# Key tiles of the exponentials added on GpSimd, weight sums two beats behind the scores

## The reference

```python
L = jnp.einsum('bhqd,bhkd->bhqk', q, k) * scale
mask = jnp.tril(jnp.ones((t, t), dtype=L.dtype))[None, None]
k_y = _split_heads(x @ w_ky.T)
L_y = jnp.einsum('bhqd,bhkd->bhqk', q, k_y) * scale
agg = jnp.sum(jnp.exp(jnp.clip(L_y, -15.0, 15.0)) * mask, axis=-1, keepdims=True) + EPS
r = _eml(L, agg)                       # log(|L| + eps) - log(agg + eps)
w = jax.nn.softplus(r) * mask
A = w / (jnp.sum(w, axis=-1, keepdims=True) + EPS)
out = jnp.einsum('bhqk,bhkd->bhqd', A, v)
```

## Time and profile before

| what | value |
|---|---|
| median of 3 runs | 1399.82 us |
| the profiled execution: its time, its span | 1398.2 us, 1396.4 us |
| TensorE matmul busy | 1280.9 us (92%) |
| VectorE, ScalarE busy | 718.2 us (51%), 614.8 us (44%) |
| GpSimd busy | 113.3 us (8%) |
| granted TensorE clock, mean | 0.972 |

### The profile page before, as it was taken

The page is one execution under the profiler, slowest core; times in us unless marked ns, Lnnn a source line. Parts: engine busy times, 40 slices in busy tenths (PEclk is TensorE's granted clock), DMA queues, the critical chain, the costliest instruction groups (busy, mean ns, idle before and its releaser), DMA issues.

```text
span 1396.4 us, 22945 instructions
## 1 busy us (share of the span) xinstructions
PE 1280.9 (92%) x8310; PEld 817.6 (59%) x8310; DVE 718.2 (51%) x1223; ACT 614.8 (44%) x810; POOL 113.3 (8%) x140
## 2 busy tenths in 40 slices
PE   5888999999898989977399999999999999999996
PEld 1433444434343434433278778787787878878785
DVE  2456777677676776566243532535326353353523
ACT  3566666666666666655042322323223241232411
POOL 1111121111111121110000000000000000000000
PEclk8999999999999999998589999999999999999998
DMA  2002222132122221000290000000000000000000
GB/s 74 16 16 69 92 75 77 60 102 78 60 90 90 90 71 57 1 31 31 70 331 15 16 15 15 30 15 19 11 15 30 15 30 0 15 30 15 30 0 16
DMA packets 31943, 66.89 MB, mean 48 GB/s; under 512 B 2848, under 2 KB 8608, under 8 KB 31904
## 3 DMA queue, kind: packets, MB, share of 16 engines
q1 hardware_dynamic: 31904, 66.35, 14.3%
HBM read 46.42 MB, written 19.92 MB: 48 GB/s over the span
## 4 chain that ended last, share of the span: by engine, by line
issue 50%; POOL 0%; DVE 0%; POOLq 0%; DVEq 0%
POOL f_rstd L809 0%; DVE f_res L816 0%; POOLq L909 0%; DVEq L821 0%; POOL f_minus_half L907 0%; POOLq L83 0%
## 5 line engine op out<-in xcount | busy, mean ns | idle before, releaser
L935 ACT ACTIVATE f_h_full<-f_layer_bank,f_scales 128x512 f32<-128x512 f32 x128 | 88.0, 687 | 354.8 <-PE f_layer_bank L1049 354.7
L500 DVE TENSOR_TENSOR w_ring<-score_banks,keep 128x1024 int32<-128x1024 int32 (+1 forms) x192 | 191.6, 1040 | 46.9 <-PE score_banks L649 46.9
L353 ACT ACTIVATE e_ring<-score_banks 128x1024 f32<-128x1024 f32 (+1 forms) x192 | 158.8, 879 | 122.8 <-PE score_banks L649 122.0
L1049 PE MATMUL f_layer_bank<-f_ha_hi,f_w_all 128*128 128x512 f32 x512 | 204.7, 400 | 2.7 <-DVE f_h_full L977 2.3
L1049 PE MATMUL f_layer_bank<-f_hb_hi,f_w_all 128*128 128x512 f32 x512 | 202.8, 396 | 0.0
L1049 PE MATMUL f_layer_bank<-f_ha_lo,f_w_all 128*128 128x512 f32 x512 | 202.1, 395 | 0.0
L1049 PE MATMUL f_layer_bank<-f_hb_lo,f_w_all 128*128 128x512 f32 x512 | 202.0, 395 | 0.0
L491 DVE TENSOR_SCALAR e_ring<-e_ring 128x2048 f32<-128x2048 f32 (+1 forms) x96 | 100.5, 1046 | 122.3 <-ACT e_ring L353 122.3
L360 ACT ACTIVATE w_ring<-w_ring 128x2048 f32<-128x2048 f32 (+1 forms) x96 | 156.8, 1633 | 8.6 <-DVE w_ring L500 8.3
L287 POOL TENSOR_SCALAR_AFFINE_SELECT e_ring<-e_ring 128x512 f32<-128x512 f32 (+1 forms) x96 | 78.5, 818 | 516.5 <-DVE e_ring L491 516.5
L675 PE MATMUL acc_bank<-w_ring,v_aug 128*32 128x512 f32 (+3 forms) x1024 | 91.2, 452 | 27.8 <-ACT w_ring L360 27.8
(11 more groups left out here) (101 smaller groups left out, 1535.0 us busy)
## 6 DMA issues: line engine op xcount, KB each, us to landing
piece<-in_wf SPq DMA_DIRECT2D x44, 256.0 KB, 2.9
wf_copy<-piece SPq DMA_DIRECT2D x44, 256.0 KB, 3.0
f_w_all<-wf_copy SPq DMA_DIRECT2D x2, 4096.0 KB, 26.4
f_x_turn<-x SPq DMA_DIRECT2D x9, 512.0 KB, 3.2
xq<-in_xt SPq DMA_DIRECT2D x8, 512.0 KB, 3.3
xv<-in_xt SPq DMA_DIRECT2D x8, 512.0 KB, 3.3
res<-in_xn SPq DMA_DIRECT2D x8, 512.0 KB, 4.6
x<-res SPq DMA_DIRECT2D x8, 512.0 KB, 2.6
```

Source lines behind the costliest of these rows:

```text
L353: nc.scalar.activation(e_ring[:, t % RING, 2 * i:2 * i + 2, 0:cols], pair_banks(y_pair(t, i), cols), ACT.Exp).then_inc(exp_done, 1)
L500: nc.vector.tensor_tensor(w_ring[:, t % RING, 2 * i:2 * i + 2, 0:cols].bitcast(I32), pair_banks(w_pair(t, i), cols).bitcast(I32), keep[:, ...
L935: nc.scalar.activation(h_full[m % 2][:], f_bank[m % RING][:], ACT.Gelu, scale=scales[:, 1 + layer, m:m + 1]).then_inc(gelu_done, 1)
L1049: mm = nc.tensor.matmul(out, left.bitcast(dt), right.bitcast(dt), start=first and n == 0, stop=last and n == 1)
```

## The change

GpSimd now adds the key tiles of the exponentials. Chunk 0 of a quad is written straight into one half of `e_sum`, chunks 1 and 2 into `e_more1` and `e_more2`, and after masking each of these GpSimd adds its tiles onto the columns of `e_sum` that see them (three adds a quad, of 4x128, 4x384 and 4x256 columns). TensorE sums the quad's exponentials with one pass of 512 columns (4 matmuls) in place of the passes over the three chunks (16 matmuls). The weights are summed at the beat t+2 instead of t+1, and ahead of `scores_w` instead of at the end of the beat. The order of the other work inside a beat is written anew on TensorE, ScalarE and VectorE.

```diff
+            def add_keys(k, t):
+                added = 3 * quad_of(k, t) + (0, 0, 2)[t % CHUNKS]
+                reach(pool, e_masked, y_beat(k, t) + 1)
+                for n, (at, j) in enumerate(CHUNK_TILES[t % CHUNKS]):
+                    reach(pool, e_added, added + n)
+                    queries = e_sum[:, t // CHUNKS, :, P * j:T]
+                    nc.gpsimd.tensor_tensor(queries, queries, exps_of(t)[:, :, at:at + T - P * j], ALU.add).then_inc(e_added, 1)
...
@@ ScalarE, exps
-                reach(act, e_summed, y_beat(k, t) - RING + 1)
+                if t % CHUNKS == 0:
+                    reach(act, e_summed, quad_of(k, t) - 1)
+                else:
+                    reach(act, e_added, 3 * quad_of(k, t) + t % CHUNKS - 2)
...
@@ ScalarE, slot (its order in a beat after the change)
+                    if y:
+                        exps(k, t)
+                    if t == 0 and 3 in w:
+                        v_sum_keep(k.shift(-1))
+                    if t == 1 and out is not None:
+                        turn_keep(out, 1)
+                    if t == 1 and any(before):
+                        copy_sums(k.shift(-1), 1, before)
+                    if t == 3 and 3 in w:
+                        base_make(k.shift(-1))
+                    if t == 4 and project:
+                        q_keep(k.shift(1))
+                    if t == 4 and (y or 0 in w):
+                        copy_sums(k, 0, (y, 0 in w))
+                    if t == 5 and y:
+                        v_keep(k)
+                    if (t - 1 in w) if t else before[1]:
+                        logs(last, m)
+                    if t == 0 and out is not None:
+                        turn_keep(out, 0)
+                    if t == 1 and before[1]:
+                        keep_att(k.shift(-1), 1, before[0])
...
@@ VectorE, slot
-                    if t == 1 and before[0]:
-                        keep_agg(k.shift(-1), 1)
-                        factors(k.shift(-1))
-                    if t == 2 and 3 in w:
+                    if t == 3 and 3 in w:
                         qc_make(k.shift(-1))
...
+                    if t == 1 and before[0]:
+                        keep_agg(k.shift(-1), 1)
+                        factors(k.shift(-1))
+                    if t == 4 and y:
+                        keep_agg(k, 0)
...
@@ TensorE
+            def sum_exps(k, g, alone):
+                reach(pe, e_added, 3 * (2 * k.index + g + 1))
+                if alone:
+                    reach(pe, acc_copied, 2 * k.index + g)
+                for r in range(QUAD):
+                    mm = nc.tensor.matmul(acc[lanes(r), :], sum_exp[:], e_sum[:, g, r, :], start=alone, stop=True)
+                mm.then_inc(e_summed, 1)
...
+                    summed, m = beat_back(k, t, 2)
+                    exps_too = before[0] if t == 1 else t == 4 and y
+                    if weights_in(t, w, before):
+                        sum_weights(summed, m, m % CHUNKS == CHUNKS - 1 and not exps_too)
+                    if exps_too:
+                        sum_exps(summed, m // CHUNKS, not weights_in(t, w, before))
+                    if t in w:
+                        scores_w(k, t, y)
```

More of the change, by code:

```diff
@@ L306, in slot @@
                         mask_e(k, t)
+                    if y and t % CHUNKS:
+                        add_keys(k, t)
                     if t == 0 and norm is not None:
@@ L384, in copy_sums @@
                 if sums[0]:
[L385 removed]
+                    reach(act, e_summed, 2 * k.index + g + 1)
                 if sums[1]:
@@ L411, in slot @@
                 for t in range(BEATS):
-                    sums = sums_of(t, y, w, before)
+                    last, m = beat_back(k, t, 1)
                     if y:
@@ L571, in slot @@
                 for t in range(BEATS):
-                    if t == 1 and before[0]:
-                        keep_agg(k.shift(-1), 1)
-                        factors(k.shift(-1))
-                    if t == 2 and 3 in w:
+                    if t == 3 and 3 in w:
                         qc_make(k.shift(-1))
-                    if t == 3 and out is not None:
-                        residual(out, 1)
-                    if t == 4 and y:
-                        keep_agg(k, 0)
                     if t == 1 and norm is not None:
@@ L751, in slot @@
                 for t in range(BEATS):
-                    sums = sums_of(t, y, w, before)
-                    last = beat_before(k, t)
                     if y:
@@ L757, in slot @@
                         sum_values(k.shift(-1))
+                    if t == 1 and out is not None:
+                        turn(out, 1)
+                    if t == 2 and out is not None:
+                        project_out(out, 0)
+                    if t == 3 and out is not None:
+                        project_out(out, 1)
+                    if t == 4 and project:
+                        q_proj(k.shift(1))
+                    if t == 5 and y:
+                        v_proj(k)
+                    summed, m = beat_back(k, t, 2)
[6 more added lines that the diff above has]
+                        scores_w(k, t, y)
+                    if t == 0 and out is not None:
+                        turn(out, 0)
                     if t == 1 and any(before):
@@ L761, in slot @@
                         spread_c(k.shift(-1))
-                    if t == 3 and out is not None:
-                        project_out(out, 1)
+                    if t == 3 and project:
+                        ky_proj(k.shift(1))
                     if t == 4 and (y or 0 in w):
@@ L766, in slot @@
                     if t == 5 and y:
-                        v_proj(k)
-                    if sums[0]:
-                        sum_exps(*last, not sums[1])
-                    if t in w:
-                        scores_w(k, t, y)
-                    if t in (0, 1) and out is not None:
-                        turn(out, t)
-                    if t == 2 and out is not None:
-                        project_out(out, 0)
-                    if t == 3 and project:
-                        ky_proj(k.shift(1))
-                    if t == 4 and project:
-                        q_proj(k.shift(1))
-                    if t == 5 and y:
                         k_proj(k)
-                    if sums[1]:
-                        sum_weights(*last, not sums[0])
             pe.wait_ge(kind_made, 3 * 2 * DT)
```

79 lines of the change are left out of this document (34 added, 45 removed).

## The result

The changed kernel takes 1466.11 us (median of 4 runs, 1465.73 to 1467.92), the kernel before 1399.63 (4 runs). The ratio is 1.048, with a 95% interval of 1.046 to 1.051: slower by 66.5 us, where 47 were forecast. The profiled execution of the changed kernel has a span of 1464.2 us, against 1396.4. Executions more than 1.5% above the fastest of their kernel, at a lower granted clock, are left out of all ratios and intervals: one of the kernel before beside experiments 1, 2, 3 and 7, and two of the ten in experiment 10.

The account below looks back on a forecast made before the run. Not TensorE's total but two chains from scores_y to the next were taken as the bound. Slots with VectorE held add 30 + 22 = 52 us, the first two slots -5: 1445 profiled, 1447 median; range 1395 to 1462.

Parts of the forecast that it names:

- The order: Beat-by-beat sum of the loop's new work order: half 0 slots +2.4 us, half 1 slots -0.6.
- The walk without a hold: Whole kernel if GpSimd's adds do not disturb VectorE: +5 us, 1404; chance 0.27.
- The swaps named there: In the beats, new TensorE waits: output projection and v_proj for att_raw, second output projection for qc.
- rival 2: Whole kernel: TensorE really is the bound, so its removed time is gained: 1350, or 1375 for half; chance 0.17.
- The hold: VectorE's SBUF steps after beat 1's absolutes wait for GpSimd's add: half 0 +2.6 us, half 1 +3.4; chance 0.50.
- The beats: Times of a slot's six beats with VectorE held by GpSimd's adds: 44.7 us half 0, 41.9 half 1.
- The granted clock is no term: Loop pass: clock ran at 0.98 and TensorE would still be busy over 80%, so no time was charged.
- In the first two slots ... mostly gained: Start of the loop: removed sums, 3.1 us each slot, mostly gained: -5 us, bounds 0 and -6.5.
- The long add: GpSimd's second add of chunk 1, 1536 columns: 2.81 us, from the slope of two rows.
- a sign of being wrong: Prediction's own check on GpSimd: it is wrong if the 1536-column add isn't near 2.8 us.
- Rival 3: GpSimd's adds cost more than the two rows' slope, a quarter dearer: +10 us, 1457; chance 0.06.
- The last slots: End of the kernel's slots: the change was to cost or gain nothing there.

Follow-up runs that it names:

- experiment 1: Changed kernel with each GpSimd add cut to one column a head: 1405.28 us, ratio 1.002 to the kernel before.
- 2: Changed kernel's new order without GpSimd's adds, TensorE summing the exponentials of every chunk two beats behind: 1442.59 us, ratio 1.031 to the kernel before.
- experiment 3: Changed kernel with each GpSimd add cut into four, one per head, over the same columns: 1450.58 us, ratio 1.037 to the kernel before.
- experiment 7: Changed kernel with 16 extra zero-adding matmuls where TensorE waits, in slots with output projections: 1461.95 us, ratio 1.045 to the kernel before.
- experiment 10: Kernel before, in its own order, with one pass of sums a quad and each GpSimd add cut to one column a head: 1407.51 us, ratio 1.005.
- 4: Changed kernel with c_spread made by four VectorE reductions instead of one copy: 1470.54 us, ratio 1.052 to the kernel before.
- 5: Changed kernel with only the long add of chunk 1 cut to one column a head: 1424.87 us, ratio 1.021 to the kernel before.
- experiment 6: Changed kernel with only the add of chunk 2 cut to one column a head: 1449.20 us, ratio 1.038 to the kernel before.
- experiment 11: Kernel before with only the first beat's exponentials' sum moved behind scores_w, no GpSimd adds: 1392.76 us against 1398.48, ratio 0.997.

## Why the prediction was right and wrong

- **The order: right beat by beat, its total partly luck.** The walk without a hold gave +5 us; experiment 1 measured +6 by the medians. In its profiled execution (1411.09 us, the longest of seven) errors cancel: the five passes are 3.7 us longer than before where 9 were forecast, the first two slots 2.2 longer where they were to be 5 shorter, and from the last full slot on it is 6.5 longer instead of 0.6 shorter. Behind the first pass its slots take 41.1 and 37.2 to 37.8 us, where the walk says 42.1 and 38.5. The first beat of the changed kernel repeats it: `scores_y` at 337.12, `scores_w` at 341.58, 4.46 later as forecast, and the next `scores_y` at 344.07, 6.95 later as forecast. The swaps named there are in the trace: the output projection waits 1.00 for `att_raw`, the second one 1.66 for `qc` (rows above), `v_proj` 0.92 for `att_raw`. That TensorE is the bound (rival 2) is refuted by experiment 1.
- **The hold: right in kind.** The row grows by what is left of the add, is bounded by the add's length (experiment 3), passes to the next instruction when its bearer is immune (4), and vanishes with the add (5). Shared bandwidth would explain the last of these, but not the first three. The rule of the Trainium skill (SBUF — State Buffer, "SBUF: two separate sides"), by which one engine is fully blocked for an instruction, agrees, with 3.10 us for a copy of 0.43. What it says of a VectorE with two SBUF inputs agrees as well: the compare is held.
- **The beats.** With the hold, half 0, forecast 6.95, 5.75, 8.1, 9.5, 7.05, 7.35; measured 6.95, 5.60, 7.99, 12.59, 6.93, 7.17. Half 1: 41.9 forecast, 41.5 measured. Two errors cancel in this, too. Against experiment 1 the adds cost a half 1 slot 3.7 to 4.3 us, where 3.4 were forecast, and a half 0 slot at full clock (44.3 in experiment 7) 3.2 for 2.6; the walk under them was 0.7 to 1.3 too dear.
- **The step that failed: "The granted clock is no term".** In beat 3 of half 0 it is one of 3 us. From 361.40, where `qc` releases the projection, full speed takes 1.92 + 1.00 + 1.07 + 1.92 by the earlier trace rows: 5.91, and the beat would have ended at 367.3, 9.65 long. It ended at 370.25. The reason given, a TensorE busy over 80% of a pass, is true of the mean over a pass (72.2 of 88.7) and says nothing of beat 2, where it was 63%. Over the five passes from 159.76 to 603.34 the kernel lost 51 us where 39 were forecast, and 5 times 2.5 is what the half 0 slots are over their 44.7. With the clock kept up in that beat (experiment 7) the same five passes are 40 us longer than before.
- **"In the first two slots ... mostly gained": wrong.** -5 was forecast, +3.2 measured (57.85 us from the first scores to those of the third slot before, 61.04 after). Experiment 1 has 60.06 there with no hold and three passes in one, so 7 of the missing 8 us do not come from the adds' length. Here, too, the clock is a term: in the second slot it was 0.85 in the changed kernel and 0.84 in experiment 1, against 1.00 before, and beat 3 took 8.76 and 8.26 us, against 5.74. Three TensorE rows of it in experiment 1 (2.09, 2.09 and 2.92 for 1.14, 1.14 and 1.98) are 2.8 us longer together. The holds (clips of 0.69 that took 3.65 and 3.92) add the last 1 us.
- **The long add: too small.** 2.81 was forecast, 3.44 measured, which the prediction had named as a sign of being wrong. Both rows it came from are multiplications with one operand spread by broadcast, 1024 columns in 1.93; an add with two full operands of as many columns takes 2.35. Rival 3 had the size and the reason (its 3.4 from the Trainium skill, GPSIMD Engine Reference, "Elementwise — side-by-side cycle accounting", agrees with 3.44), priced at +10 us. In the held beats the longer add was offset by the walk that was too dear (7.99 for 8.1, 41.5 for 41.9), so it is not seen in the 19 us.
- **The last slots: "nothing" was wrong by 4.** From the start of the last full slot to the end 812.4 us became 819.1, of which 2.8 were forecast for that slot. Experiment 1 has 819.0 there with nothing held, so it is not the adds. Up to the first TensorE row of the next phase (`f_out_bank`) it is 106.5 us before, 111.6 in experiment 1 and 112.5 after; what in the new order or the clock costs it there stays open.

The ledger: +47.4 forecast in the profiled execution, +67.8 measured. The difference of 20 is +8 in the first two slots, +12 in the five passes, -3 in the next slot, +4 at the end and -0.5 ahead of the first. Of these, the 12 go when the clock is kept up in beat 3 (7), and most of the 8 and the 4 are there without any hold (1). What stays open is how much the clock owns outside the passes: it falls elsewhere when one beat is mended (6, 7), and no experiment kept it up over the whole kernel.

## What to carry to other kernels

Moving work to GpSimd is not free where it fills memory that VectorE also works on: list what VectorE does in each add's lifetime, and place the adds beside its reads of PSUM, or on no one's way to the next scores. Before removing work from the busiest engine, find on which side of the waited-for instruction it stands; work that fills a wait can be worth nothing, and moving one sum by one place (experiment 11) gained what removing two of three did not. And read the granted clock of the single stage, not of the pass, as soon as a change makes TensorE wait in it.

## What the runs showed of the hardware

- While GpSimd's add ran, VectorE's copy, clip and two-input compare were held to its end. Reciprocal (0.55 us), the reduction (0.28), the statistics (1.40 for four at 378.25 in the changed kernel, beside adds from 376.10 to 380.90) and the absolutes, which read PSUM (1.29 for the two of chunk 2 at 358.43 in experiment 4, beside the add from 358.56), were not.
- It works the other way too: a mask of 0.68 took 1.66 when it met a clip (the mask from 32.23, the clip from 31.19 to 33.36 us in the changed kernel).
- GpSimd's add costs 1.29, 2.35 and 3.44 us for 512, 1024 and 1536 columns: 2.1 ns a column and 0.2 fixed. Four adds of 384 columns took 4.70, 1.26 more than the one of 1536; by the fixed part only 0.6 of that would come, as an estimate, and the rest is unexplained.
- TensorE at the lower level of 1.2 GHz nearly doubles its rows (1.99 to 3.78, 1.14 to 2.09). With the long stall removed at one place, the low clock appeared at another of the same slot (0.92 and 0.89 on either side of a beat at 1.00, experiment 6).
